# Small self-attention on packed probabilities: blocks of 32x32 turned on VectorE, products on parts of the TensorE array, and each result bank with its own counter

## The chip, the cores and the metric

The kernel runs on one core of one Trainium2 chip. Its engines are TensorE (PE, with its weight loads listed apart as PEld), VectorE (DVE), ScalarE (ACT), GpSimd (POOL) and SyncE (SP), each with its own instruction stream; they meet at semaphores, which are counters that one engine raises and another waits for. The metric is the time of one execution on the device, in microseconds (us). The kernel before takes 1611.82 us, the median of three runs (1604.68 to 1613.89).

## What is computed

A block of three layers on `x` (64 sequences of 32 rows, 256 wide), all in float32 at the interface:

```python
x = x + xattn(_layernorm(x), ctx_1024)   # 16 heads of 128, 257 keys for each sequence, rmsnorm on q and k
x = x + attn(_layernorm(x))              # 16 heads of 16, 4 key/value heads, rotary, causal over 32 rows
x = x + ffn(_layernorm(x))               # 8 experts, the best one for each row, plus a shared expert
```

The middle layer is the one that the change rewrites:

```python
scores = jnp.einsum('bqhgd,bkhd->bhgqk', qg, k) * scale
scores = jnp.where(causal, scores, -inf)
attn = jax.nn.softmax(scores, axis=-1)
y = jnp.einsum('bhgqk,bkhd->bqhgd', attn, v).reshape(bsz, seqlen, dim)
return ternary_linear(rms_norm(y), w_proj)
```

## The kernel before

The 2048 rows are worked on as 16 tiles of 128 rows, so a tile holds four sequences (`NB` = 4) of 32 rows. The program has a prologue (`pro`, which prepares weights and starts tile 0), 15 `full` periods, a `last` period and four `expert` periods. One full period does the early half of the next tile (cross attention) and the late half of this one (the end of the cross attention, the small self-attention, the shared expert, the routing). Each engine has a list of step names in `ORDER` for a period, and issues the steps in that order; nothing else sets the order. An engine waits at a step until its operands are counted as ready, and everything behind it on the same engine waits too.

The steps that matter here. `K0` to `K7` are the key products of the cross attention (12 matmuls of 512 columns each, into the four banks of `AB`); ACT squares two of the banks and DVE takes statistics of the other two. `Q`, `QP` and `f` are other large products. For sequence `b` of the tile: `rk{b}` turns and spreads the key norms into `C`; `s{b}` are its scores, into `AB`; `e{b}` (ACT) the exponentials; `i{b}` (DVE) the inverse sums; `n{b}` (POOL) scales the probabilities; `pt{b}` (PE) turns them into `C` and the last key's into `Db`; `ph{b}` and `tl{b}` (ACT) copy these out, `dp{b}` (DVE) writes the low half; `o{b}` (PE) is the product with the context, into `Eb`; `oh{b}` and `do{b}` drain it; `c{b}` (POOL) splits the context rows that `o{b}` multiplies. `h{b}` (POOL) splits the context that the next tile's `K` steps need, and `scat` (POOL) sends the tile's rows to the experts.

The small self-attention is `qk` (turns the heads), `sc` (16 products with 16 rows of contraction, of all 128 rows of the tile with all 128, of which only the four diagonal blocks of 32x32 are used), the mask on DVE (`sc`), the exponentials on ACT (`sc`), which write the four blocks of each head into `px`, a 128x2048 array that is zero elsewhere, `pt` (PE turns the 16 heads of `px`, 128x128 each, ACT and DVE copy them to `pxT`), `pv` (16 products of `pxT` with 17 columns, the last of which gives the sums), `yt` (turns `y`), and `pr` (the projection).

PSUM is divided into the four banks of `AB` (counters 0 to 3), `C` (two banks, one counter), `Db` and `Eb`. `filled` counts what PE has written there, `drained` what has been read out. Line 587 is the helper through which nearly all products go, line 924 the squares of the keys, line 1281 the statistics of the keys.

## Time and profile before

| | us |
|---|---|
| median of 3 runs | 1611.82 |
| lowest and highest | 1604.68, 1613.89 |
| the profiled execution | 1609.09 |
| its span, first to last instruction | 1607.3 |
| mean granted TensorE clock | 0.946 |

PE is busy for 86% of the span, DVE for 65%, ACT for 54% and POOL for 34%. A busy PE is not PE at its peak: the end of a matmul is modelled, and a matmul at half the clock is as busy as one at the full clock. The profile names for each idle time the engine that ended it.

### The profile page before, as it was taken

The page shows a single profiled execution, that of the slowest core. Times are in us where ns is not written, and L with a number is a line of the kernel's source. Part 1 is how long each engine was busy: PE and PEld are TensorE (multiplying, and loading weights), DVE is VectorE, ACT ScalarE, POOL GpSimd, SP SyncE. Part 2 cuts the span into 40 slices and gives each one's busy share as a digit, 9 for nine tenths or more (in the row PEclk, how much of TensorE's full clock was granted, in tenths as well). Part 3 has the DMA queues.
Part 4 walks back from the last instruction along what each step waited for, and adds up shares of the span by engine and source line. Part 5 has one row for each costly group of instructions (what it writes and reads, how often), then busy time and mean ns, then how long its engine had stood idle before and what let it go on. Part 6 is the DMA issues. An engine that isn't in the chain of part 4 may idle for free.

```text
span 1607.3 us, 32866 instructions
## 1 busy us (share of the span) xinstructions
PE 1378.4 (86%) x9178; PEld 956.8 (60%) x9178; DVE 1044.2 (65%) x3905; ACT 864.9 (54%) x3432; POOL 540.7 (34%) x1338
## 2 busy tenths in 40 slices
PE   5859989998989898989999998989898989955882
PEld 2635757565756666665757565756666665734661
DVE  6836767676767676777767676767676777733112
ACT  5455656566565656565565566565656565621110
POOL 2143333334243525243343334342525243300003
PEclk9989999999999999999998999999999999976896
DMA  9010000000000001010000000000101010100544
GB/s 372 4 28 8 26 17 21 13 27 13 24 17 14 27 10 30 10 30 7 24 17 21 13 25 15 24 17 10 30 10 30 7 33 3 59 6 19 163 127 134
DMA packets 41190, 59.63 MB, mean 37 GB/s; under 512 B 5094, under 2 KB 35953, under 8 KB 40096
## 3 DMA queue, kind: packets, MB, share of 16 engines
q1 hardware_dynamic: 36880, 50.73, 9.9%
q0 software_dynamic: 2064, 6.14, 1.2%
q10 hardware_dynamic: 2176, 2.10, 0.4%
q14 instruction: 59, 0.48, 0.1%
q8 instruction: 11, 0.18, 0.0%
HBM read 48.62 MB, written 10.49 MB: 37 GB/s over the span
## 4 chain that ended last, share of the span: by engine, by line
PE 57%; issue 14%; POOL 10%; DVE 9%; ACT 7%; DMA 3%; POOLq 1%; SPq 0%; DVEq 0%; ACTq 0%
PE AB L587 30%; PE Eb L587 9%; PE Db L587 5%; PE C L720 3%; PE C L587 3%; ACT px L1003 2%; DMA ctxn<-expert_rows 2%; POOL prob L1140 2%; PE AB L783 2%; POOL c_lo L1105 2%; PE C L704 2%; DVE sc L1509 1%; ACT AB L924 1%; POOL c_hi L1103 1%; POOL pjunk L1099 1%
## 5 line engine op out<-in xcount | busy, mean ns | idle before, releaser
L924 ACT ACTIVATE AB<-AB 128x128 f32<-128x128 f32 (+1 forms) x1160 | 302.8, 261 | 180.8 <-PE AB L587 175.8
L1099 POOL TENSOR_TENSOR pjunk<-pjunk 128x1 f32<-128x1 f32 x288 | 55.9, 194 | 703.2 <-DVE sinv L1443 341.3
L1281 DVE BATCH_NORM_STATS2 kst<-AB 128x6 f32<-128x256 f32 x512 | 182.1, 417 | 71.3 <-PE AB L587 64.9
L587 PE MATMUL AB<-wk_hi,c_hi 128*128 128x512 f16 x512 | 205.2, 401 | 20.8 <-DVE sc L1509 10.0
L924 ACT ACTIVATION_READ_ACCUMULATOR AB<-AB 128x1 f32 (+1 forms) x1160 | 215.4, 186 | 0.0
L587 PE MATMUL AB<-wk_lo,c_hi 128*128 128x512 f16 x512 | 204.0, 398 | 0.0
L587 PE MATMUL AB<-wk_hi,c_lo 128*128 128x512 f16 x512 | 203.0, 396 | 0.0
L993 ACT ACTIVATE prob<-prob,nbias,rq 128x257 f32<-128x257 f32 x256 | 150.6, 590 | 39.8 <-DVE nbias L1438 39.4
L1140 POOL TENSOR_SCALAR prob<-prob,sinv 128x257 f32<-128x257 f32 x256 | 123.8, 484 | 20.1
L587 PE MATMUL AB<-ctxT,qpT 128*128 128x257 f32 x512 | 127.3, 392 | 0.2 <-DVE kst L1281 0.2
L962 ACT CAST pT<-C 128x1024 f16<-128x1024 f32 x64 | 64.5, 1008 | 80.4 <-PE C L720 80.4
L587 PE MATMUL Eb<-pT,cn_hi 128*128 128x512 f16 x256 | 78.8, 390 | 33.6 <-DVE pT L1447 33.6
L587 PEld LDWEIGHTS AB<-ctxT,qpT 128*128 128x128 f32 x512 | 96.0, 196 | 16.6 <-DVE kst L1281 1.0
L720 PE MATMUL C<-consts_sb,prob 128*128 128x128 f32 x512 | 71.9, 286 | 38.4 <-POOL plast L1150 21.9
L587 PEld LDWEIGHTS AB<-wk_hi,c_hi 128*128 128x128 f16 x512 | 52.0, 102 | 88.2 <-issue 18.4
L1432 DVE CUSTOM_DVE_ANT_0 prob<-AB,rkb 128x257 f32<-128x257 f32 x256 | 96.2, 421 | 10.4 <-issue 9.2
L1116 POOL TENSOR_TENSOR rstd<-var,minus_half 128x1 f32<-128x1 f32 x64 | 35.3, 552 | 190.0 <-DVE var L1266 155.5
L587 PEld LDWEIGHTS AB<-wk_hi,c_lo 128*128 128x128 f16 x512 | 52.3, 102 | 67.2 <-issue 12.1
L720 PEld LDWEIGHTS C<-consts_sb,prob 128*128 128x128 f32 x512 | 58.8, 148 | 55.2 <-ACT rkb L987 23.7
L587 PE MATMUL Db<-wvo_hi,o_halves 128*128 128x256 f16 x512 | 88.2, 276 | 1.4 <-DVE o_halves L1453 1.4
L1447 DVE TENSOR_TENSOR pT<-C,pT 128x1024 f16<-128x1024 f32 x64 | 77.9, 1217 | 15.6 <-ACT pT L962 15.1
L587 PE MATMUL AB<-x_hi,wqk_hi 128*128 128x128 f16 x512 | 86.6, 219 | 0.0
(253 smaller groups left out, 3240.7 us busy)
## 6 DMA issues: line engine op xcount, KB each, us to landing
ctxT<-in_ctxT SPq DMA_DIRECT2D x64, 128.5 KB, 2.1
ctxn<-in_ctxn SPq DMA_DIRECT2D x64, 128.0 KB, 2.1
wq_hi<-in_w SPq DMA_DIRECT2D x4, 768.0 KB, 4.9
wq_lo<-in_w SPq DMA_DIRECT2D x4, 768.0 KB, 6.2
expert_rows<-base POOLq DMA_DIRECT2D x1, 2048.0 KB, 15.7
xin<-in_x SPq DMA_DIRECT2D x16, 128.0 KB, 2.2
prob<-in_wqT SPq DMA_DIRECT2D x1, 2048.0 KB, 19.1
xres<-in_x SPq DMA_DIRECT2D x16, 128.0 KB, 2.0
```

Source lines behind the costliest of these rows:

```text
L587: return pe.matmul(out, lhsT, rhs, start=start, stop=stop)
L704: ins = pe.transpose(C[:, g // 2, KT * P * (g % 2) + P * tt:KT * P * (g % 2) + P * (tt + 1)], rkx[:, b % 2, tt, P * g:P * (g + 1)], ident)
L720: ins = pe.transpose(C[:, tt, P * g:P * (g + 1)], prob[:, b, g, P * tt:P * (tt + 1)], ident)
L924: ins = nc.scalar.activation(k, k, ACT.Square, accum_out=sums[0:m, h:h + 1])
L962: nc.scalar.copy(pT[:, b % 2, 0].rearrange("p t n -> p (t n)"), C[:].rearrange("p a n -> p (a n)"))\
L993: ins = nc.scalar.activation(prob[:, b, g], prob[:, b, g], ACT.Exp, bias=nbias[:, b, g:g + 1], scale=rq[:, G * b + g:G * b + g + 1], accum ...
L1099: own.mark(pool.tensor_tensor(pjunk[:, 0:1], pjunk[:, 1:2], pjunk[:, 1:2], ALU.mult))
L1116: pool.tensor_tensor(rstd[:, n:n + 1], var[:, n:n + 1], minus_half[:], ALU.pow)\
L1140: ins = pool.tensor_scalar(prob[:, b, g], prob[:, b, g], sinv[:, b, g:g + 1], P_SCALE, ALU.mult, ALU.mult)
L1281: ins = V.bn_stats(stats[:, 0, 2 * half + n], AB[0:m, 2 + half, 2 * D * n:2 * D * (n + 1)])
L1432: V.tensor_tensor_reduce(prob[:, b, g], AB[:, g, 0:SKV], rkb[:, b % 2, g], 1.0, BELOW, ALU.mult, ALU.max, smax[:, b, g:g + 1]).then_inc(dr ...
L1447: V.tensor_tensor(all_of(pT[:, b % 2, 1]), all_of(C[:]), all_of(pT[:, b % 2, 0]), ALU.subtract)\
```

## The change

1. The probabilities are kept packed: `ex`, 128 rows by 16 heads by 32 keys (128x512, a part of `px`). One exponential writes them. DVE then sums them, divides them (before, the division came behind the product), and turns them with one instruction that transposes each 32x32 block (`step_sm`). The 16 turns on PE, the 128x512 copies of them and the zeros of `px` are gone.
2. `pv` is 16 products with 32 rows of contraction and 32 columns of weights over 128 columns, each on its own 32x32 part of the array: sequence `b` gives the rows and the bank, the key/value head `kv` the columns. The result is `y` already turned, so `yt` is gone. ACT copies it out (four copies) and squares it; DVE adds the squares of the four groups; PE sums over the rows (`st`); DVE and POOL make the norm's factor. Since 16 of every 32 rows of `y` turned are empty, `pr` has four products of 256 columns in place of two, and the weights `wproj` are laid out with gaps by the prologue (`wpad`).
3. `sc` issues its 16 products with the four groups of rows in turn (before: four products of one group, then the next).
4. The two banks of `C` have counters of their own, 4 and 5, and `rk`, `pt`, `qk`, `up` and their drains go bank by bank.
5. `o{b}`, `f` and `Q` first issue the products that need only the high halves, and wait for the low halves behind them.
6. The first two integer steps of `newton` become one.
7. The step lists are written anew.

```diff
 "PE":
-    K0 pt3 K1 K2 X K3 o3 Q f rk0 K4 xt1 K5 qkv QP K6 qk s0 rk1 sc K7 s1 pt pv pt0 s2 yt pr rk2 o0 pt1
-              xt2 s3 lg up pos o1 rk3 pt2 dn o2
+    K0 K1 K2 pt3 X K3 o3 Q f K4 rk0 xt1 K5 qkv QP K6 s0 qk sc rk1 K7 s1 pt0 pv pr st s2 rk2 o0 pt1 xt2
+              s3 lg o1 up pos rk3 dn pt2 o2
...
 "POOL":
-    h2 h0 h3 h1 n3 X r0 ln1 cl r1 c0 c2 c1 n0 r2 y n1 ln2 c3 r3 n2 scat
+    h0 h1 n3 X h2 c0 h3 r0 cl c1 r1 ln1 n0 r2 y n1 ln2 r3 c3 n2 scat c2
...
 (PE, attend)
                 for tt in range(KT):
+                    pe.wait_ge(ph_ready[tt].sem, ph_ready[tt].at(p, f"ph{b}"))
                     mm(Eb[:], cn_hi[:, b, tt], pT[:, b % 2, 0, tt], start=tt == 0, stop=False)
+                    mm(Eb[:], cn_lo[:, b, tt], pT[:, b % 2, 0, tt], start=False, stop=False)
+                for tt, s in enumerate("45"):
+                    pe.wait_ge(drained[s].sem, drained[s].at(p, f"pt{b}"))
                     mm(Eb[:], cn_hi[:, b, tt], pT[:, b % 2, 1, tt], start=False, stop=False)
-                    mm(Eb[:], cn_lo[:, b, tt], pT[:, b % 2, 0, tt], start=False, stop=False)
...
 (PE, step_pv)
-                for n, s in enumerate(BANKS):
-                    pe.wait_ge(drained[s].sem, drained[s].at(p, "pt"))
-                    for h in range(4 * n, 4 * n + 4):
-                        ins = mm(Eb[:, (AD + 1) * h:(AD + 1) * (h + 1)], pxT[:, h], vals[:, h % AKV])
+                probs = exT.rearrange("p i (kv q) -> p i kv q", kv=AKV)
+                for kv in range(AKV):
+                    for b, s in enumerate(BANKS):
+                        rows = slice(SQ * b, SQ * (b + 1))
+                        ins = mm(AB[SQ * kv:SQ * (kv + 1), b, 0:P], vals[rows, kv], probs[rows, :, kv])
...
 (ACT, step_sc)
-                for b in range(NB):
-                    rows = slice(SQ * b, SQ * (b + 1))
-                    ins = nc.scalar.activation(px[rows, :, SQ * b:SQ * (b + 1)], sc[rows], ACT.Exp)
+                nc.scalar.activation(all_of(ex), all_of(sc[:]), ACT.Exp).then_inc(ex_ready.sem, 1)
...
 (ACT, step_pv)
+                for b, s in enumerate(BANKS):
+                    act.wait_ge(filled[s].sem, filled[s].at(p, "pv"))
+                    ins = nc.scalar.copy(yT.rearrange("p i (b q) -> p b i q", b=NB)[:, b],
+                                         AB[:, b, 0:P].rearrange("p (i q) -> p i q", q=SQ))
+                    ins.then_inc(drained[s].sem, 1)
+                for s in BANKS:
+                    act.wait_ge(drained[s].sem, drained[s].at(p, "pv"))
+                nc.scalar.activation(all_of(ysq), all_of(yT), ACT.Square).then_inc(ysq_ready.sem, 1)
...
 (DVE, step_sm)
+                step(V.tensor_reduce(psum[:], by_key, AX.X, ALU.add))
+                step(V.reciprocal(prec[:], psum[:]))
+                step(V.tensor_tensor(by_key, by_key, prec[:].unsqueeze(2).broadcast_to([P, AH, SQ]), ALU.mult))
+                V.transpose(all_of(exT), all_of(ex)).then_inc(exT_ready.sem, 1)
```

How the order moves at three places. On PE in the middle of a full period, before: from the scores `s1` (the first row) over the turns of `px`, `pv` and `pt0` to the scores `s2`.

```order
L587 MATMUL AB<-ctxT,qpT 128x257 x4
L779 REGISTER_ALU
L781 REGISTER_ALU
L783 MATMUL AB<-consts_sb,px 128x128 x16
L789 REGISTER_ALU
L587 MATMUL Eb<-vals,pxT 128x17 x16
L715 REGISTER_ALU
L717 REGISTER_ALU x2
L720 MATMUL C<-consts_sb,prob 128x128 x8
L587 MATMUL Db<-ident,plast 12x128 x4
L587 MATMUL AB<-ctxT,qpT 128x257 x4
```

The same stretch of the changed kernel, from `s1` to `s2`.

```order
L593 MATMUL AB<-ctxT,qpT 128x257 x4
L729 REGISTER_ALU
L731 REGISTER_ALU
L733 MATMUL C<-consts_sb,prob 128x128 x8
L735 REGISTER_ALU
L593 MATMUL Db<-ident,plast 12x128 x4
L590 REGISTER_ALU
L593 MATMUL AB<-pxT,vals 32x128 x16
L816 REGISTER_ALU
L593 MATMUL Eb<-wproj,pxT 128x256 x4
L593 MATMUL Db<-ones,px 128x1
L593 MATMUL AB<-ctxT,qpT 128x257 x4
```

`pt0` has moved ahead of the small attention's product and now stands directly behind `s1`; `pr` and the sum of squares stand ahead of `s2`.

On ACT, in the same part of the period, before: from the exponentials of the small attention to the copy of `y` turned.

```order
L1003 ACTIVATE px<-sc 32x16x32 x4
L915 REGISTER_ALU
L916 COPY pxT<-AB 128x512 x2
L991 REGISTER_ALU
L993 ACTIVATE prob,ssum<-prob,nbias,rq 128x257 x4
L961 REGISTER_ALU
L962 CAST pT<-C 128x1024
L915 REGISTER_ALU
L916 CAST pTl<-Db 12x512
L915 REGISTER_ALU
L916 COPY yT<-Db 128x256
```

The same part of the changed kernel.

```order
L1023 ACTIVATE px<-sc 128x512
L1009 REGISTER_ALU
L1010 COPY rkb<-C 128x2x256 x2
L937 REGISTER_ALU
L938 CAST pTl<-Db 12x512
L984 REGISTER_ALU
L985 CAST pT<-C 128x512 x2
L1040 REGISTER_ALU
L1041 COPY pxT<-AB 128x4x32 x4
L1046 ACTIVATE px<-pxT 128x512
L1014 REGISTER_ALU
L1016 ACTIVATE prob,ssum<-prob,nbias,rq 128x257 x4
```

The exponentials `e1` of sequence 1 (the row with `prob,ssum`) have moved from ahead of the copies of `pT` to behind them and behind the copies and squares of `y`.

On PE at the end of a full period, before: from `rk3` over `pt2` and `dn` to the first products of `o2`.

```order
L704 MATMUL C<-consts_sb,rkx 128x128 x8
L717 REGISTER_ALU
L720 MATMUL C<-consts_sb,prob 128x128 x8
L587 MATMUL Db<-ident,plast 12x128 x4
L584 REGISTER_ALU
L587 MATMUL Eb<-sw,hT 128x256 x3
L728 REGISTER_ALU
L584 REGISTER_ALU
L735 REGISTER_ALU
L587 MATMUL Eb<-pT,cn_hi 128x512 x2
L587 MATMUL Eb<-pT,cn_lo 128x512
```

The same place of the changed kernel.

```order
L718 MATMUL C<-consts_sb,rkx 128x128 x8
L590 REGISTER_ALU
L593 MATMUL Eb<-sw,hT 128x256 x3
L731 REGISTER_ALU
L733 MATMUL C<-consts_sb,prob 128x128 x8
L593 MATMUL Db<-ident,plast 12x128 x4
L590 REGISTER_ALU
L747 REGISTER_ALU
L593 MATMUL Eb<-pT,cn_hi 128x512
L593 MATMUL Eb<-pT,cn_lo 128x512
L593 MATMUL Eb<-pT,cn_hi 128x512
L593 MATMUL Eb<-pT,cn_lo 128x512
```

`dn` (the row with `sw,hT`) now stands between `rk3` and `pt2`, and `o2` begins with the products of the high half.

## Rows read from the trace of the kernel before

**Rows 1.** The page: busy time of each engine, its share of the span, and its instructions.

```profile
PE 1378.4 (86%) x9178; PEld 956.8 (60%) x9178; DVE 1044.2 (65%) x3905; ACT 864.9 (54%) x3432; POOL 540.7 (34%) x1338
```

**Rows 2.** Instructions on `px`: count, duration in ns, first and last start in us.

```profile
L783 PE MATMUL AB<-consts_sb,px x256: 272/273/477, 179.2 to 1459.8; 128*128 128x128 f32 x128
```

**Rows 3.** Timeline of PE in one period: start, us, instruction, idle before and its releaser.

```profile
678.43 1.04 PE L766 MATMUL C<-consts_sb,heads 128*128 128x128 f32 x8
...
682.01 2.81 PE L587 MATMUL AB<-wt_q 16*128 16x128 f32 x32
...
692.02 1.97 PE L783 MATMUL AB<-consts_sb,px 128*128 128x128 f32 x16 [0.68 <-ACT px L1003]
693.82 3.64 PE L587 MATMUL Eb<-vals,pxT 128*128 128x17 f32 x32
697.31 1.07 PE L720 MATMUL C<-consts_sb,prob 128*128 128x128 f32 x8
...
701.31 1.13 PE L587 MATMUL Eb<-wproj,yT 128*128 128x256 f32 x4 [0.46 <-ACT yT L916]
...
704.71 1.06 PE L720 MATMUL C<-consts_sb,prob 128*128 128x128 f32 x8
```

**Rows 4.** Who PE waited for from 606.6 to 692 us, one period: us, times, longest.

```profile
PE Eb L587 <- DVE pT L1447: 1.9, 1, 1.9
PE C L720 <- ACT rkb L987: 1.1, 1, 1.1
PE Eb L596 <- DVE xn L1270: 1.0, 1, 1.0
...
PE AB L783 <- ACT px L1003: 0.7, 1, 0.7
PE C L720 <- POOL plast L1150: 0.6, 1, 0.6
```

**Rows 5.** Stretches of that period: length, busy time of the engines, granted clock, DMA.

```profile
686.00:688.00 2.00, 2.00 (x6) 0.64 (x5) 1.83 (x6) 1.04 (x9) 0.00 (x0) 0.50 0.00 0
...
694.00:696.00 2.00, 2.00 (x21) 2.00 (x20) 1.83 (x8) 2.00 (x7) 0.00 (x0) 1.00 0.54 177
```

**Rows 6.** Timeline of DVE from the mask of the small scores to `i0`.

```profile
683.82 3.63 DVE L1509 TENSOR_TENSOR sc<-AB,consts_sb 32x256 f32<-32x256 f32 x10 [1.19 <-PE AB L587]
...
688.31 0.69 DVE L1522 TENSOR_TENSOR sc<-sc,scm 128x512 f32<-128x512 f32 x1
689.03 1.43 DVE L1281 BATCH_NORM_STATS2 kst<-AB 128x6 f32<-128x256 f32 x4
690.37 0.16 DVE L1443 RECIPROCAL sinv<-ssum 128x4 f32<-128x4 f32 x1
```

**Rows 7.** Timeline of ACT: the copy of the turned heads, exponentials, copies of `pT` and `pTl`.

```profile
679.51 1.01 ACT L916 COPY wt_q<-C 128x1024 f32<-128x1024 f32 x1 [0.48 <-PE C L766]
...
695.58 0.59 ACT L993 ACTIVATE prob<-prob,nbias,rq 128x257 f32<-128x257 f32 x1
...
698.42 1.01 ACT L962 CAST pT<-C 128x1024 f16<-128x1024 f32 x1 [2.16 <-PE C L720]
699.33 0.57 ACT L916 CAST pTl<-Db 12x512 f16<-12x512 f32 x1
```

**Rows 8.** Timeline of POOL: the scaling of the probabilities (`n0`), and the next one's start.

```profile
690.90 2.15 POOL L1140 TENSOR_SCALAR prob<-prob,sinv 128x257 f32<-128x257 f32 x4
...
693.57 0.22 POOL L1150 TENSOR_TENSOR plast<-prob,plast 128x4 f16<-128x4 f32 x1
...
701.29 0.19 POOL L1099 TENSOR_TENSOR pjunk<-pjunk 128x1 f32<-128x1 f32 x1 [0.59 <-DVE sinv L1443]
```

**Rows 9.** Timeline of POOL at a period's end: a context split, the scatter.

```profile
620.16 0.67 POOL L1160 TENSOR_TENSOR cn_lo<-ctxn,cn_hi 128x256 f16<-128x256 f32 x1
...
630.92 1.12 POOL L1181 DMA_INDIRECT expert_rows<-xn,slot_s  x1 [0.58 <-issue]
```

**Rows 10.** Timeline of ACT in the last period: the four exponentials.

```profile
1454.13 2.54 ACT L1003 ACTIVATE px<-sc 32x512 f32<-32x512 f32 x4 [8.67 <-DVE sc L1522]
```

More of the change, by code:

```diff
@@ L763, in step_qk @@
                 pe.wait_ge(heads_ready.sem, heads_ready.at(p, "h"))
-                start(p, "qk")
-                for m in range(2 * AKV):
-                    ins = pe.transpose(C[:, m // 4, P * (m % 4):P * (m % 4 + 1)], heads[:, m], ident)
-                ins.then_inc(filled["C"].sem, 1)
+                for n, s in enumerate("45"):
+                    pe.wait_ge(drained[s].sem, drained[s].turn(p, "qk"))
+                    for m in range(AKV * n, AKV * (n + 1)):
+                        ins = pe.transpose(C[:, n, P * (m % 4):P * (m % 4 + 1)], heads[:, m], ident)
+                    ins.then_inc(filled[s].sem, 1)
```

270 lines of the change are left out of this document (144 added, 126 removed).

## The prediction

> **What bounds the kernel now.** I read the page first. PE is busy for 86% of the span, DVE for 65%, ACT for 54%, POOL for 34% [rows 1]. The turns of `px` come once in a tile, from 179.2 to 1459.8 us [rows 2]: 15 intervals of 85.4 us, so the full periods are 80% of the time, and what a period gains counts fifteen times. Then the waits of PE in one period [rows 4]: 1.9 for `pT`, 1.1 for `rkb`, 1.0 for `xn`, 0.7 for `px`, 0.6 for `plast` and a few smaller, 7 of 85 us. So PE is the bound, but narrowly: the reader should see that each of these waits is the end of a chain through DVE, ACT and POOL, and that work taken from PE becomes time only until the next chain is late. So I follow the chains.
>
> **PE's ledger.** In the timeline [rows 3] the turns of `px` run from 692.02 to 693.82 (1.8 us) and the old `pv` to 697.31 (3.5). With the turns of `y` (0.2) that is 5.5 us a period that go. The 16 products of `sc` take 2.81. DVE begins its mask, which needs the first 8 of them, at 683.82 [rows 6], so 8 take at most 1.8 us, 0.22 each; all 16 take 0.18 each, so the groups of rows overlap a little already where one follows the other. Issued in turn they should overlap throughout: between a quarter (16 x 0.22 / 4 = 0.9) and no change (2.8). I take 1.3, nearer the quarter, because of the overlap that the row shows. The new `pv` is 16 such products, with 32 columns of weights: 0.9 to 3.6 (the old `pv`'s pace, 32 entries of 0.11 us); I take 1.4 for the same reason. `pr` has four products of 256 columns for two: its row is 1.13, so it takes about 2.0, +1.0; `st` is 0.15. Ledger: -5.5 - 1.5 + 1.4 + 1.0 + 0.15 = -4.4 us a period, 66 us in fifteen.
>
> The TensorE page of the Trainium skill (Part 3, Packing small matmuls) gives 3.07 times the speed for four groups of rows. By that `sc` would take about 1.15 us, an estimate from the page, and the sum would move by 0.15 us a period.
>
> **Stage 1, `K0` to `K6`: gain 1.2.** `pt3` now stands behind `K2`, and POOL does `n3` behind two context splits in place of four: the 0.6 for `plast` goes. The 1.0 for `xn` is DVE arriving late at `f`; `do3` has moved behind `KN0` and `Q`, `newton` is one step shorter, `f` starts without waiting for the low halves, and `K4` rather than `rk0` plus `K4` stands behind it with the same length in all. I leave 0.4 of it. What DVE queues behind `do3` is `RQ`, which `i0` and the biases need much later.
>
> **Stage 2, from the end of `K6` (678.43) to `pt1` (704.71, so 26.3 us): gain 1.2, or a loss of 0.6.** Times are from the end of `K6`. `s0` now goes before `qk`, so `sc` has nothing to cover ACT's copy of the heads (1.01 in one piece [rows 7], now two, the first overlapped): PE stands about 0.8, `sc` starts at 3.4 (before 3.6) and is done at 4.8. The mask takes 3.6, the maximum and the subtraction 1.4, the statistics of `K7` 1.4, `i0` 0.16 [rows 6]: `i0` is done at 11.5, before 12.1. So the shorter `sc` is worth 0.6 here, not 1.5: the chain on DVE is the limit. POOL's `n0` takes 690.61 to 693.79, 3.2 [rows 8], so `pt0` can start at 14.8; PE has only `s1` to do until then and **stands idle for 2.8 us**, where before it stood 0.7. This is a new wait, and it eats most of the ledger. Meanwhile DVE does `step_sm`: the sum and the product are 128x512 like the row of 0.69, the reciprocal 0.2; the transposition is not in the trace; its bounds are one such pass (0.69) and two (1.4), and I take one, since it reads and writes 128x512 once. Then `s1` (2.2) ends at 16.1, when `pt0` does. With two passes `pv` would start 0.7 later.
>
> `pv` ends at 17.5. ACT first copies `pTl` and `pT` (0.57 and two halves of 1.01 [rows 7]), then the four banks of `y`: 1024 columns take 1.01 and 512 take 0.57, so 128 take 0.25, four 1.0 to 1.2. `pr` starts at 18.8: **another 1.3 of PE idle**. Then `pr` 2.0, `st` (the squares on ACT 0.6 and DVE's sum 0.7 are behind `pr` by then), `s2`, `rk2`, `o0`: 25.0. On ACT `e1` stands behind all this (squares to 19.4, then four exponentials of 0.59), `i1` at 22, and POOL's `n1` takes 3.2: `pt1` at 25.1. Two chains end together, against 26.3 before. That is the gain of 1.2.
>
> **The clock.** The granted clock is 0.50, the 1.2 GHz level, at 686 to 688 us in each period, behind the products of 16 rows, and 1.00 at 694 to 696, in the old `pv` [rows 5]. In the changed kernel the stretch from `s1` to `pr` holds 4.1 us of idle time, 8 turns and 16 products that use a sixteenth of the array each, less than what stood before the drop in `sc`. I expect a second drop there in each period. At half the clock `pt0` costs 1.3 more (all behind it moves), and `pr` and `s2` 0.5 beyond what the chain through `e1` hides: +1.8. The first drop stays, under `K7`, where DVE's mask is slower anyway.
>
> **Stage 3, from `pt1` to the next `K0`: gain 2.0.** 1.1 (`rkb`) goes since `dn` now covers ACT's copy. Of the 1.9 for `pT` most goes, as `o2` starts on the high halves. What is late next is POOL: `c2` (0.40 and 0.67 and a gate, 1.3 [rows 9]) now stands behind the scatter, `o2` needs it, and the scatter needs DVE's `up` and `pos`. From the end of `up` I count 2.2 to the slots, 2.1 to the scatter's end, 1.3 for `c2`, 1.5 for `o2`: 7.1. Before it was 10.4, of which `o1` (1.5) is now ahead of `up`. Gain 1.8 to 2.0, bounds 0 and 3.0 (both waits gone).
>
> **Outside the periods.** The last period is a bare chain at half the clock: one exponential for four (2.54 to about 0.65 [rows 10]), masks that start earlier (1.3), no turns of `px` and `y`, but `pr` takes 4 and the norm's factor comes 1.4 behind it: about -3. The prologue gains a zeroing, two copies and four turns on DVE and PE, +1 (0 to 3); the zeroing of `px` that POOL loses was beside other work. The experts are not touched.
>
> **Sum.** 1.2 - 0.6 + 2.0 = 2.6 a period, 39 in fifteen, and 2 outside: 1609.1 - 41 = 1568 in terms of the profiled execution. The median of the runs shown is 2.7 above that execution, so 1571.
>
> **Rivals.**
> *No second drop.* The old `pv` kept the full clock with 17 columns a product, and the wait for `pT` did not lower it. Then stage 2 gains 1.2, 4.4 in all: 66 + 2, 1543.
> *Narrow products that do not overlap.* All 16 loads and products run in a row: `pv` 3.6, so +2.2 from `pt0` to `pr`, half hidden where the clock's 1.8 is already partly under it; I count +1.5 a period: 1593. For it: the old `pv` ran at its loads' pace, 0.11 each. Against it: the 0.18 of `sc`. The same TensorE page (LDWEIGHTS) says that a load's time goes by its columns and not by its rows, which would speak for this in `sc`, where the columns stay 128; this trace shows loads of 16 rows, but in one group at a time.
> *The edits cancel.* If stages 1 and 3 give 0.6 in place of 3.2 (POOL's and DVE's chains late at `K0` and `xt1`), nothing is left: 1610.
> *Slower.* One mechanism: the path `pt0`, ACT's copies, `pv`, `e1`, `n1` carries both the serial products (+2.2) and half the clock over `pt0`, `pv`, `pr` and `s2` in two drops (+3.4 in place of 1.8), 3.8 more than in the forecast. It decides from 2.6 more. Then a period is 1.2 longer: +18 - 2, about 1627. For it: two new PE waits on this very path. Against: it needs both.
> *The whole ledger arrives.* Waits covered, 4.4 + 3.0 a period: about 1498. Against: the idle time before `pt0` is fixed by DVE and POOL.
>
> **How the numbers follow.** Forecast 0.45 (1571), no second drop 0.18 (1543), no overlap 0.14 (1593), cancel 0.09, slower 0.10, the whole ledger 0.04. The range 1538 to 1608 leaves out the ledger and the slower case and takes in the bound of stage 3 on both sides. A measurement here tells 0.5% (8 us). Faster by more than that: 0.45 + 0.18 + 0.14 + 0.04 and a little of the cancel case, 0.82; within 0.08; slower 0.10.
>
> **What would show it.** The pitch of a period (about 82.8; 81 without the second drop); the wait before `pt0` for `plast`, near 2.8; a wait of `pr` for ACT's copies, near 1.3; 16 products of `pv` in about 1.4 us and of `sc` in 1.3; a second stretch of granted clock 0.50 in each period between `pt0` and `s2`; the waits for `pT` and `rkb` at the period's end gone and one for `cn` in their place. The prediction is wrong if the pitch is over 85, or if PE does not wait before `pt0`.

## The result, and the profile after

The changed kernel takes 1627.61 us (median of 4 runs, 1625.00 to 1630.07), against 1609.78 us for the kernel before beside it. The ratio is 1.0112, with a 95% interval of 1.0076 to 1.0148: slower by 1.1%, where 1571 us was forecast. The profiled execution has a span of 1628.3 us and a mean granted clock of 0.917 (before 1607.3 and 0.946).

The page of the changed kernel, busy times, answers to [rows 1]:

```profile
PE 1321.8 (81%) x8990; PEld 885.9 (54%) x8990; DVE 1059.9 (65%) x3844; ACT 842.5 (52%) x3560; POOL 542.5 (33%) x1337
```

PE is busy for 57 us less, and the span is 21 us longer. So the work was taken off PE as planned and did not become time. The waits of PE in the whole run of the changed kernel (engine, tile and line, who ended the wait: us in total, times, longest):

```profile
PE C L733 <- POOL plast L1183: 61.7, 19, 6.6
PE Eb L602 <- DVE xn L1297: 39.0, 16, 2.6
PE Eb L593 <- ACT pxT L1041: 28.0, 16, 1.8
PE Eb L593 <- POOL cn_lo L1193: 21.4, 15, 1.5
```

and the same list of the kernel before:

```profile
PE Eb L587 <- DVE pT L1447: 33.6, 17, 2.6
PE C L720 <- POOL plast L1150: 21.9, 18, 5.9
PE Eb L596 <- DVE xn L1270: 18.2, 16, 2.5
...
PE C L720 <- ACT rkb L987: 16.5, 15, 1.1
```

The waits for `pT` and `rkb` are gone as forecast. Those for `plast` and `xn` have grown by 61 us together, the two below them in the list are new, and one for `wt_q` (16.9 us in all) as well. The granted clock over five periods, before and then after (stretch, length, busy time of PE, PEld, DVE, ACT and POOL with counts, clock, DMA share, GB/s):

```profile
333.00:755.00 422.00, 386.18 (x2653) 264.58 (x2651) 303.00 (x1173) 256.95 (x1050) 158.08 (x401) 0.98 0.07 19
```

```profile
333.00:755.00 422.00, 363.08 (x2575) 240.19 (x2574) 297.48 (x1112) 247.46 (x1062) 155.87 (x394) 0.93 0.06 19
```

A mean of 0.98 is 17 us of 422 at the lower level (1.2 GHz), 0.93 is 59 us. Before, each of these periods has one stretch at that level, under `K7`. In the changed kernel the clock under `K7` is 1.00 in every period, and the lower level comes in 9 of 15 periods behind the wait for `xn`, and in all of them from the wait in front of `pt0` on. Here is the changed kernel's second stage on PE, which answers to [rows 3] (start, duration, instruction, idle time before it and its releaser):

```profile
701.87 1.17 PE L593 MATMUL AB<-wt_q 16*128 16x128 f32 x32 [1.12 <-ACT wt_q L938]
702.98 1.09 PE L718 MATMUL C<-consts_sb,rkx 128*128 128x128 f32 x8
...
713.78 1.97 PE L733 MATMUL C<-consts_sb,prob 128*128 128x128 f32 x8 [3.24 <-POOL plast L1183]
715.67 0.59 PE L593 MATMUL Db<-ident,plast 128*12 128x128 f16 x4
716.20 0.73 PE L593 MATMUL AB<-pxT,vals 32*32 32x128 f32 x32
718.71 3.75 PE L593 MATMUL Eb<-wproj,pxT 128*128 128x256 f32 x8 [1.78 <-ACT pxT L1041]
722.26 0.43 PE L593 MATMUL Db<-ones,px 128*128 128x1 f32 x2
...
726.86 1.04 PE L733 MATMUL C<-consts_sb,prob 128*128 128x128 f32 x8
```

The narrow products are as quick as hoped: `sc` fell from 2.81 to 1.17 us, and the new `pv` takes 0.73. Around them PE stands: 3.24 in front of `pt0`, 1.78 in front of `pr`. From `pt0` to `pr` the clock is at its lower level:

```profile
719.00:721.00 2.00, 2.00 (x6) 1.55 (x6) 1.76 (x3) 2.00 (x8) 0.00 (x0) 0.50 0.00 0
```

so `pt0` takes 1.97 where `pt1` takes 1.04, and `pr` 3.75.

**Where the time went**, from the two timelines, in the period I followed. From `K0` to `Q`, 0.8 less. From `Q` to the end of `K6`, 3.1 more. From there to `pt1`, 29.2 against 26.3: 2.9 more. From `pt1` to the next `K0`, 15.5 against 17.7: 2.2 less. This period lost 3.0; they are not all alike. Over the 14 intervals from the first `Q` of a full period to the last the mean went from 85.9 to 87.5, 23 us in all; in this mean the four parts are 0.7 less, 2.5 more, 2.0 more and 2.1 less. Outside them the time up to that first `Q` is 3.2 longer, the stretch from the last `Q` to the last `dn` 8.0 shorter and the end behind it 2.5 longer: 2 us less, and the sum is the 21 of the spans. The 3.2 is not the change's: i0_first and dense_fill run the same program up to that point, and reach it 4.1 us earlier than the changed kernel and 0.9 earlier than the one before. The 2.5 at the end is no clearer (121.8 to 129.5 us over all the runs below, 126.7 before, 129.3 in the changed kernel). So the question is what `Q` to `K6` and `K6` to `pt1` lose.

### The profile page after: what moved, and what is told of

It is laid out like the page before. It is cut to its first block, busy times and chain, and to the rows that moved or that the text cites. A ratio compares the mean times of both kernels' runs of the same rounds, so it can differ in the third digit from the quotient of the medians.

```text
span 1628.3 us, 32714 instructions
## 1 busy us (share of the span) xinstructions
PE 1321.8 (81%) x8990; PEld 885.9 (54%) x8990; DVE 1059.9 (65%) x3844; ACT 842.5 (52%) x3560; POOL 542.5 (33%) x1337
## 4 chain that ended last, share of the span: by engine, by line
PE 36%; issue 22%; POOL 18%; ACT 7%; DVE 6%; DMA 3%; POOLq 1%; SPq 0%; DVEq 0%; ACTq 0%
PE AB L593 17%; PE Eb L593 7%; PE Db L593 5%; POOL prob L1173 4%; ACT AB L946 3%; PE C L733 3%; PE C L593 2%; POOL pjunk L1128 2%; DMA ctxn<-expert_rows 2%; POOL rkx L1164 2%; POOL c_lo L1134 2%; DVE sc L1544 1%; DVE kst L1308 1%; POOL c_hi L1132 1%; ACT pT L985 1%
## 5 line engine op out<-in xcount | busy, mean ns | idle before, releaser
L593 PE MATMUL AB<-wk_hi,c_hi 128*128 128x512 f16 x512 | 201.5, 394 | 28.4 <-DVE sc L1544 16.3
L593 PE MATMUL AB<-ctxT,qpT 128*128 128x257 f32 x512 | 134.6, 393 | 4.0 <-DVE kst L1308 3.2
L1173 POOL TENSOR_SCALAR prob<-prob,sinv 128x257 f32<-128x257 f32 x256 | 130.6, 510 | 20.2
L733 PE MATMUL C<-consts_sb,prob 128*128 128x128 f32 x512 | 77.9, 302 | 61.7 <-POOL plast L1183 61.7
L593 PEld LDWEIGHTS AB<-ctxT,qpT 128*128 128x128 f32 x512 | 91.6, 191 | 34.1 <-DVE kst L1308 14.7
L1010 ACT COPY rkb<-C 128x512 f32<-128x512 f32 x128 | 68.0, 583 | 78.7 <-PE C L718 78.7
L733 PEld LDWEIGHTS C<-consts_sb,prob 128*128 128x128 f32 x512 | 64.6, 154 | 79.4 <-issue 59.9
L593 PE MATMUL Eb<-pT,cn_hi 128*128 128x512 f16 x256 | 87.9, 384 | 22.9 <-POOL cn_lo L1193 21.4
L1483 DVE TENSOR_TENSOR pT<-C,pT 128x512 f16<-128x512 f32 x128 | 81.7, 677 | 10.9 <-ACT pT L985 10.9
L938 ACT CAST pTl<-Db 12x512 f16<-12x512 f32 x64 | 36.7, 573 | 100.5 <-PE Db L593 100.5
L593 PEld LDWEIGHTS AB<-wk_hi,c_lo 128*128 128x128 f16 x512 | 51.5, 101 | 64.7 <-issue 7.6
```

The lines of the kernel that those rows point to most:

```text
L593: return pe.matmul(out, lhsT, rhs, start=start, stop=stop)
L733: ins = pe.transpose(C[:, tt, P * g:P * (g + 1)], prob[:, b, g, P * tt:P * (tt + 1)], ident)
L938: nc.scalar.copy(out, in_).then_inc(drained[s].sem, 1)
L1010: nc.scalar.copy(rkb[:, b % 2, 2 * n:2 * n + 2, 0:KT * P], C[:, n].rearrange("p (g n) -> p g n", g=2)).then_inc(drained[s].sem, 1)
L1173: ins = pool.tensor_scalar(prob[:, b, g], prob[:, b, g], sinv[:, b, g:g + 1], P_SCALE, ALU.mult, ALU.mult)
L1483: V.tensor_tensor(pT[:, b % 2, 1, tt], C[:, tt], pT[:, b % 2, 0, tt], ALU.subtract).then_inc(drained[s].sem, 1)
```

## Experiments

All times are medians. The ratio is to the kernel before, run beside it, with its 95% interval. The kernel before took 1609.8 us beside the changed kernel; 1615.3 beside do3_first, i0_first, both_first and dense_fill; 1612.2 beside pool_ln1, pool_i0, pool_i0_do3 and order_old; 1618.6 beside c2_ahead, c2_fill, order_old_pt0 and sc_in_turn; 1611.4 beside before_st3, before_st3_pt0 and st2_old; 1614.8 beside counters_new and counters_old. So where two runs of different groups are set against each other in us, up to 9 us may be the group, and the ratios are the safer guide.

| run | us | ratio |
|---|---|---|
| the changed kernel | 1627.6 | 1.0112 (1.0076 to 1.0148) |
| do3_first | 1640.8 | 1.0166 (1.0101 to 1.0231) |
| i0_first | 1598.2 | 0.9891 (0.9823 to 0.9959) |
| both_first | 1613.0 | 0.9997 (0.9970 to 1.0023) |
| dense_fill | 1603.0 | 0.9918 (0.9889 to 0.9948) |
| pool_ln1 | 1589.5 | 0.9833 (0.9785 to 0.9882) |
| pool_i0 | 1562.1 | 0.9674 (0.9621 to 0.9726) |
| pool_i0_do3 | 1552.7 | 0.9627 (0.9576 to 0.9678) |
| order_old | 1638.7 | 1.0143 (1.0095 to 1.0191) |
| c2_ahead | 1548.6 | 0.9562 (0.9536 to 0.9588) |
| c2_fill | 1546.3 | 0.9542 (0.9511 to 0.9573) |
| order_old_pt0 | 1640.6 | 1.0129 (1.0102 to 1.0157) |
| sc_in_turn | 1616.6 | 0.9958 (0.9921 to 0.9996) |
| before_st3 | 1635.8 | 1.0152 (1.0122 to 1.0182) |
| before_st3_pt0 | 1680.9 | 1.0427 (1.0392 to 1.0461) |
| st2_old | 1566.2 | 0.9717 (0.9692 to 0.9742) |
| counters_new | 1588.6 | 0.9834 (0.9783 to 0.9885) |
| counters_old | 1635.1 | 1.0130 (1.0081 to 1.0178) |

### Two places in the lists, and the clock

**do3_first**, on DVE:

```
-K3 KN0 Q do3 RQ f K4
+K3 do3 KN0 Q RQ f K4
```

> The changed kernel with one step moved on DVE: the low half of o3 (do3) goes back ahead of the rotation's norms KN0, where it stood before. Theory A (stage 1 is lost to this order): the chain Q stats, RQ ends 0.7 us earlier against the start of Q, TensorE's wait for xn falls from 2.4 us to under 1.5 us per period, the clock drop of 3.4 us behind it goes in most periods, and the period falls by 1.5 to 2.5 us, which over 15 periods gives 1590 to 1605 us. Rival B (the newton chain is slow for another reason, POOL's work beside it, and do3 only fills a gap): the wait for xn stays above 2 us and the time within 0.4% of 1627 us.

Both times wrong: 1640.8, 13 us above the changed kernel, and the wait for `xn` rose from 39.0 to 52.4 us in the run. Of the two causes it is rival B's, POOL's work beside DVE, that holds, as the rest shows. The step between the statistics of `Q` and `xn` was gone and `xn` came later still. That sent me to DVE's small operations there. In the kernel before, one of `newton` (a timeline of DVE):

```profile
659.22 0.18 DVE L1255 SCALAR_TENSOR_TENSOR nb_<-nc_,nb_ 128x16 f32<-128x16 f32 x1
```

The same operations on the same 128x16 numbers in the changed kernel, on DVE, and what POOL does at the time:

```profile
675.62 0.53 DVE L1280 SCALAR_TENSOR_TENSOR nc_<-nb_ 128x16 f32<-128x16 f32 x1
676.18 0.17 DVE L1281 TENSOR_TENSOR nc_<-nc_,na 128x16 f32<-128x16 f32 x1
676.39 0.60 DVE L1282 SCALAR_TENSOR_TENSOR nb_<-nc_,nb_ 128x16 f32<-128x16 f32 x1
677.02 0.52 DVE L1280 SCALAR_TENSOR_TENSOR nc_<-nb_ 128x16 f32<-128x16 f32 x1
...
678.20 0.17 DVE L1281 TENSOR_TENSOR nc_<-nc_,na 128x16 f32<-128x16 f32 x1
```

```profile
675.42 0.69 POOL L1193 TENSOR_TENSOR cn_lo<-ctxn,cn_hi 128x256 f16<-128x256 f32 x1
...
676.35 1.16 POOL L1164 COPY rkx<-rk 128x512 f32<-128x512 f32 x2
...
682.80 0.56 POOL L1148 TENSOR_TENSOR rstd<-var,minus_half 128x1 f32<-128x1 f32 x1 [5.29 <-DVE var L1293]
```

POOL's last copy of `r1` ends at 677.51, and from then on every operation of DVE takes 0.17 again. In the list of before, `ln1` stands ahead of `cl` and `r1` on POOL, so POOL was waiting for DVE through all of this. The new list has `r0 cl c1 r1 ln1`, which fills POOL's wait with copies.

The durations say more. The slow operation that starts at 676.39 ends at 676.99, and the one at 677.02 ends at 677.54, where POOL's two copies end at 676.96 and 677.51. Over the whole run 45 of the 176 operations on 128x16 numbers take more than 0.3 us, and each of the 45 ends within 0.04 us of the end of an instruction of POOL. In do3_first it is 75 of 176, again each of them, and here DVE and POOL side by side:

```profile
677.24 0.89 DVE L1277 TENSOR_SCALAR nb_<-na 128x16 int32<-128x16 int32 x1
...
678.37 1.01 DVE L1281 TENSOR_TENSOR nc_<-nc_,na 128x16 f32<-128x16 f32 x1
```

```profile
677.04 1.05 POOL L1205 TENSOR_TENSOR cl_cast<-cl_cast,low_rows 12x512 f16<-12x512 f16 x1
678.17 1.18 POOL L1208 TENSOR_TENSOR cl_rows<-ctxl,cl_cast 12x512 f16<-12x512 f32 x1
```

So the small operation is not slower work: it stands until POOL's instruction is over. None of those that take under 0.3 us lies inside an instruction of POOL that takes over 0.3. The Trainium skill (SBUF — State Buffer, SBUF: two separate sides) says that a DVE instruction with two SBUF inputs contends with a GpSimd instruction that reads SBUF, and one in a two-port mode with any, for a pair of ports that one of them holds for a whole instruction. The rows agree with the whole instruction. Two inputs are not the condition here, since L1277 has one and took 0.89; whether it runs in a two-port mode no run shows.

**pool_ln1**, on POOL:

```
-h3 r0 cl c1 r1 ln1 n0
+h3 r0 ln1 cl c1 r1 n0
```

> The changed kernel with one step moved on POOL: ln1 goes ahead of cl, c1 and r1, where it stood before, so that POOL waits for the variance of ln1 while DVE works out the rotation's scale from the statistics of Q. Theory A (stage 1 is lost to POOL's copies beside DVE's small operations: 13 operations from the statistics of Q take 4.5 us here against 2.9 us before, and 5.8 us with do3 moved ahead, since POOL's work then falls on more of them): these operations take 0.17 us each again, xn is ready 1.5 us or more earlier, the wait for xn falls from 2.4 to under 1 us, the drop in stage 1 goes, and the time is 1590 to 1612 us. Rival B (DVE's operations are slow because TensorE or ACT read and write PSUM beside them): they stay slow, the wait stays, and the time within 0.4% of 1627 us.

Theory A, at the edge of its range: 1589.5, 38 us under the changed kernel from one word in a list. DVE's operations are at 0.17 to 0.18 again:

```profile
661.74 0.18 DVE L1282 SCALAR_TENSOR_TENSOR nb_<-nc_,nb_ 128x16 f32<-128x16 f32 x1
```

and PE's wait for `xn` over the run fell from 39.0 to

```profile
PE Eb L602 <- DVE xn L1297: 16.7, 16, 2.5
```

The 22 us of wait are not all of the 38: behind the wait for `xn` the clock fell for 3.4 us in 9 of 15 periods of the changed kernel (686 to 688 us: 0.50), and those stretches are gone too. The one behind `pt0` has grown for it, and in all a period has 9.8 us at the lower level where it had 10.7.

**i0_first**, on DVE, and **both_first**, with the edit of do3_first as well:

```
-K6 s0 sc K7 i0 sm s1
+K6 s0 i0 sc K7 sm s1
```

> The changed kernel with one step moved on DVE: the reciprocal i0 of block 0's sums goes ahead of the masks of sc, from behind the eighth K. Theory A (stage 2 is lost to DVE's order: i0 stands behind 5.2 us of masks and 1.4 us of statistics, so POOL starts prob of block 0 6 us later than its input allows, TensorE stands 3.2 us in front of pt0, and the clock falls for the 10.2 us behind it): the wait for plast of block 0 goes, the second drop is gone or only behind pr, the period falls by 3.5 to 5 us, and the time is 1550 to 1575 us. Rival B (TensorE then waits the same time for the transposed probabilities of sm, which DVE gives now 0.9 us later): the wait of 3.2 us turns into one of 2 to 2.5 us in front of pv, the clock falls anyway, and the time is 1610 to 1625 us.

> The changed kernel with both moves on DVE, do3 ahead of KN0 and i0 ahead of sc. If the two losses are independent, the gains add: 1515 to 1545 us. If they are one loss through the clock, which falls once per period in any case, the time is that of the better of the two alone, within 0.5%.

i0_first took 1598.2, 29 us under the changed kernel, between the two expectations, and each had a part of it. `pt0` starts without a wait, since `n0` is now done 3.9 us ahead of it. But PE then waits in front of `pv`:

```profile
693.95 1.04 PE L733 MATMUL C<-consts_sb,prob 128*128 128x128 f32 x8
694.92 0.39 PE L593 MATMUL Db<-ident,plast 128*12 128x128 f16 x4
697.41 0.51 PE L593 MATMUL AB<-pxT,vals 32*32 32x128 f32 x32 [2.10 <-DVE smax L1467]
699.06 3.75 PE L593 MATMUL Eb<-wproj,pxT 128*128 128x256 f32 x8 [1.14 <-ACT pxT L1041]
```

`pt0` and `pv` are at the full clock (1.04 and 0.51), `pr` still at half. The wait of 2.10 is for the banks of `s1`, at the end of one unbroken row of DVE's work from the masks on. both_first gave 1613.0, 15 us above i0_first, which neither expectation has: `do3` ahead of `KN0` did the same harm as before.

**dense_fill** tests the clock by itself, with the changed kernel's order:

```
+                if b == 0 and p.kind == "full":
+                    pe.wait_ge(drained["4"].sem, drained["4"].turn(p, "pt0"))
+                    for r in range(14):
+                        mm(C[:, 0], wk_hi[:, 0:P], wk_hi[:, 0:512])
                 pe.wait_ge(p_ready.sem, p_ready.at(p, f"n{b}"))
```

> The changed kernel with 14 additional products of 128x512, whose results are overwritten, in the bank of pt0 while TensorE waits in front of pt0 (14 x 0.215 = 3.0 us in a wait of 3.2 us). They do nothing but keep TensorE busy. Theory A (the idle stretch in front of pt0 is what takes the clock away for pt0, pv, pr and s2): the granted clock stays 1.00 over these steps, pt0 takes 1.0 us and pr 2 us instead of 2.0 and 3.8, the period falls by 2 to 4 us, and the time is 1570 to 1600 us although 14 products a period were added. Rival B (the drop is set by the narrow products of sc and pv themselves): the clock falls all the same and the time is 1625 to 1640 us.

```profile
696.73 3.19 PE L593 MATMUL C<-wk_hi 128*128 128x512 f16 x14
700.07 1.09 PE L737 MATMUL C<-consts_sb,prob 128*128 128x128 f32 x8
701.09 0.39 PE L593 MATMUL Db<-ident,plast 128*12 128x128 f16 x4
701.41 0.50 PE L593 MATMUL AB<-pxT,vals 32*32 32x128 f32 x32
703.92 2.58 PE L593 MATMUL Eb<-wproj,pxT 128*128 128x256 f32 x8 [2.02 <-ACT pxT L1045]
```

Theory A in its mechanism, and 3 us outside its range: 1603.0, 25 us faster with 14 useless products more in each period. `pv` is as narrow as before, and the clock stays. So what takes the clock away from `pt0` and `pv` is the idle stretch in front of them, and that costs about 1.6 us a period (25 in fifteen). What is left of half clock there is one stretch of 3.4 us, which begins inside `pr`.

**pool_i0** and **pool_i0_do3** put the edits together: ln1 and `i0`, then `do3` as well.

> The changed kernel with ln1 ahead of cl, c1 and r1 on POOL and i0 ahead of sc on DVE. If both gains count, the period is 83 to 84 us and the time 1565 to 1585 us. Rival (the period stays near 85.3 us, where before, i0_first and dense_fill all lie in spite of different work, because time that is taken out comes back as a further stretch at half clock): 1592 to 1600 us, as i0_first.

> The changed kernel with three moves: ln1 ahead of cl, c1 and r1 on POOL, i0 ahead of sc and do3 ahead of KN0 on DVE. Theory A (do3_first was slower only because it pushed the statistics' operations under POOL's work): with POOL out of the way do3's 0.7 us leave the chain to xn, and the time is 0 to 10 us under that of pool_i0. Rival B (do3 ahead of KN0 costs by itself, since it makes rk of the first half 2 us later for POOL): slower than pool_i0 by over 8 us, as do3_first against the changed kernel (13 us) and both_first against i0_first (15 us).

Both gains count nearly in full: 1562.1 is 65.5 us under the changed kernel, where 38.1 and 29.4 make 67.5 (by the ratios 4.4% of 5.0%). And `do3` ahead of `KN0`, which cost 13 and 15 us with POOL in the way, now gains 9: 1552.7. This is theory A of that run, and it settles stage 1: it is POOL's work that holds up DVE, and `do3_first` was slower only because it pushed DVE's chain further under them. The mean interval from `Q` to `Q` is now 82.6 us, where 82.8 was forecast.

### What of the change carries the gain

**order_old**: the changed kernel with every list in the order of before, as far as the steps exist in both. **order_old_pt0**: the same, with stage 2 as in i0_first. The core of the first:

```
-K6 s0 qk sc rk1 K7 s1 pt0 pv pr st s2 rk2 o0 pt1 xt2 s3 lg o1 up pos rk3 dn pt2 o2
+K6 qk s0 rk1 sc K7 s1 pv pt0 s2 pr st rk2 o0 pt1 xt2 s3 lg up pos o1 rk3 pt2 dn o2
```

> The changed kernel, its attention with compact probabilities included, with its steps on all four engines in the order of before as far as they exist in both (on TensorE pv, pt0, s2, pr, st; on ACT sc, pv, e1, ph0, tl0; on DVE i0, sm, s1, KN1, ys, dp0, i1, yv; POOL's list as before). Theory A (the loss is in the new order, the packed attention itself gains): the half clock behind pt0 is shorter, since pv stands in the wait for plast, the period is 82 to 84.5 us and the time 1560 to 1600 us. Rival B (the packed attention itself costs what the order cannot help: DVE's chain of masks, sum, reciprocal, product and transposition, then four copies and a square on ACT before pr): the period is 86 us or more, and the time 1620 to 1650 us.

> The kernel of order_old (1638.7 us) with the second stage alone in the new order and i0 ahead of sc: on TensorE pt0, pv, pr, st, s2, on ACT tl0, ph0, pv, e1, on DVE i0, sc, K7, sm. Stages 1 and 3 stay as before. Theory A (the packed attention needs other work in the time in which DVE makes its probabilities; with pt0 there it pays): the period falls from 88.7 to 84 to 86 us, and the time is 1570 to 1605 us. Rival B (the loss of order_old lies in the variance of y, which now stands behind pr and st and holds back n1, x2 and the rest in either order): 1620 to 1640 us.

1638.7 and 1640.6 are the times of rival B, but not a proof of its cause. Both kernels also have the counters per bank and the high halves first. These alone, with the old attention in the old order, take 1635.1 (counters_old, below): 1.0130 against 1.0143 for order_old, which can't be told apart. So in the old order the packed attention itself neither gains nor costs anything that these runs can tell. The periods are 88.7 us in both kernels and 88.2 in counters_old. In order_old the trace shows three places. In front of `pv` PE stands 3.31 us (for DVE, as in i0_first), and half clock follows. The variance of `y`, which DVE used to work out from `y` itself, now waits for `pr` and `st`: POOL's factor starts 51.5 us behind `Q` where it was 48.8, and `n1`, behind it on POOL, at 52.3 where it was 50.3. And in the next period PE waits for `n3`, and the clock falls once more:

```profile
744.11 0.38 PE L593 MATMUL Eb<-pT,cn_hi 128*128 128x512 f16 x1 [0.70 <-DVE base L1634]
...
750.87 1.97 PE L733 MATMUL C<-consts_sb,prob 128*128 128x128 f32 x8 [2.43 <-POOL plast L1183]
```

This third place does not come from the packed attention. counters_old has it too, though its `n1` stands 50.3 behind `Q` as before:

```profile
746.02 1.09 PE L727 MATMUL C<-consts_sb,prob 128*128 128x128 f32 x8 [2.39 <-POOL plast L1170]
```

In these two and in the kernel before POOL starts `n3` 6.4 us behind the scatter. PE starts `K0` 6.2 us behind it in the kernel before, and 4.3 in order_old and counters_old, since its wait of 2.0 for `pT` has become one of 0.7 for `base`. `pt3` stands directly behind `K0` in the old list, so the time saved there comes back as a wait for POOL.

**sc_in_turn**: the kernel before, with `sc` alone issued in turn over its groups of rows.

```
-                    for kv in range(AKV):
-                        ins = mm(AB[:, m, P * kv:P * (kv + 1)], headsT[rows, kv], headsT[rows, AKV + kv])
-                    ins.then_inc(filled[s].sem, 1)
+                for kv in range(AKV):
+                    for m, s in enumerate(BANKS):
+                        ins = mm(AB[:, m, P * kv:P * (kv + 1)], headsT[rows, kv], headsT[rows, AKV + kv])
+                        if kv == AKV - 1:
+                            ins.then_inc(filled[s].sem, 1)
```

> The kernel before with one part of the change alone: the 32 products of sc are issued over the four groups of rows in turn and all four banks are reported at the end. Theory A (the products overlap, but what follows sc is bound by DVE's masks, so the 1.6 us that TensorE saves are not saved on the path): sc takes 1.2 us instead of 2.8, the eighth K starts at most 0.5 us earlier, and the time is within 0.5% of before. Rival B (the time saved stays, and the half clock behind sc goes with the slow narrow products): the period falls by 1.5 to 3 us, 1565 to 1590 us. Rival C (the banks come all at the end, so the masks start later and the idle stretch behind sc grows): 1615 to 1635 us.

Theory A. First `sc` and the next `K7` in the kernel before, then in this one:

```profile
682.01 2.81 PE L587 MATMUL AB<-wt_q 16*128 16x128 f32 x32
685.47 0.61 PE L587 MATMUL AB<-wk_hi,c_hi 128*128 128x512 f16 x1 [0.65 <-DVE sc L1509]
```

```profile
688.38 1.17 PE L587 MATMUL AB<-wt_q 16*128 16x128 f32 x32 [0.32 <-DVE smax L1434]
691.29 0.53 PE L587 MATMUL AB<-wk_hi,c_hi 128*128 128x512 f16 x1 [1.74 <-DVE sc L1511]
```

The 1.6 us taken from `sc` came back as a longer wait for DVE's masks: `K7` starts 34.0 us behind `Q`, before 34.2. The clock still falls under `K7` (0.50 from 692 to 694 us), so the slow narrow products were not what lowered it in the kernel before. The ratio of 0.9958 is at the edge of what can be measured.

**before_st3** has the old attention and the new order of stages 1 and 3 (with `ln1` ahead of `cl`); **before_st3_pt0** has `i0` and `pt0` early as well; **counters_old** and **counters_new** add the counters per bank of `C` and the high halves first, in the old order and in that of before_st3. Of the lists of PE and POOL in before_st3:

```
-K0 pt3 K1 K2 X ... lg up pos o1 rk3 pt2 dn o2
+K0 K1 K2 pt3 X ... lg o1 up pos rk3 dn pt2 o2
-h2 h0 h3 h1 n3 X r0 ln1 cl r1 c0 c2 c1 n0 ... c3 r3 n2 scat
+h0 h1 n3 X h2 c0 h3 r0 ln1 cl c1 r1 n0 ... r3 c3 n2 scat c2
```

> The kernel before, with its own attention (turns of px, the old pv, yt), and with the steps of the first and third stage in the order of pool_i0_do3 (K0 K1 K2 pt3 at the period's start; lg, o1, up, pos, rk3, dn, pt2, o2 at its end; oh0 ahead of tl1; lg ahead of up on ACT; h0 h1 n3 and scat, c2 on POOL; ln1 ahead of cl). Theory A (the gain that stays is stage 3's order, 3.0 of 3.3 us a period, and the packed attention gives nothing): the period falls to 82 to 83 us and the time is 1550 to 1572 us, within 1% of pool_i0_do3. Theory B (the packed attention is needed: without it the new order meets a longer second stage, and the time comes back as half clock): 1590 to 1615 us.

> The kernel of before_st3 with stage 2 changed too, still with the old attention: i0 ahead of sc on DVE, pt0 ahead of the turns of px on TensorE, tl0 and ph0 ahead of the copies of px on ACT. Theory A (pt0 early fills the wait for px and costs nothing): 0 to 8 us under before_st3. Theory B (i0 delays the masks by 0.7 us, and the masks are what the turns of px wait for): 0 to 15 us above before_st3.

> The kernel of before_st3 (old attention, new order of stages 1 and 3 with ln1 ahead of cl) with the change's counters per bank of C and its products that start with the high halves. So it is the changed kernel in its mended form without the packed attention and without the new order of stage 2. Theory A (counters, high halves and stage 3's order together are the whole gain that stays; the packed attention gives nothing): the waits for pT and hT go, the period is 81.5 to 83 us, and the time 1540 to 1562 us, at or under pool_i0_do3's 1552.7. Theory B (the packed attention gives its share): 1570 to 1590 us, above pool_i0_do3 by over 1%.

> The kernel before, its attention and its order as they were, with the counters per bank of C and the products that start with the high halves alone. Theory A (in the old order nothing waits for the low halves, since other work stands between them, so finer counters find no wait to shorten): within 0.7% of before, 1600 to 1615 us. Theory B (they shorten waits in any order): 1570 to 1595 us.

Theory A fell in all four, and theory B holds in counters_new alone. The new order alone costs 1.5% (1635.8), and PE's waits in before_st3 say why:

```profile
PE Eb L587 <- DVE pT L1447: 47.7, 23, 2.8
PE C L704 <- DVE hT L1572: 21.2, 15, 1.4
```

With `o1` right behind `lg`, and `rk3` right behind `up`, PE meets the low half of `pT` and the second bank of `C` before they are done. The counters per bank and the high halves first take away these two waits (68.9 us; one of 21.4 for `c2` takes their place). Alone in the old order they cost 1.3% (1635.1: the wait for `pT` is gone, and that for `plast` is 46.2 us in place of 21.9, as above). Together they give 1588.6, 1.7% faster than before. So neither part would have been kept if tried alone. The packed attention takes the 1588.6 to 1566.2 (st2_old, below). In before_st3_pt0 `pt0` early with the old attention cost a further 45 us, three times the most that theory B allowed; its trace has PE waiting 32.1 us for `sc` on DVE, as theory B has it, against 12.5, and 10.2 us a period at the lower clock against 5.6. Which of its moves brings the clock down was not tested.

**st2_old**: pool_i0_do3 with stage 2 alone in the old order.

```
-K6 s0 qk sc rk1 K7 s1 pt0 pv pr st s2 rk2
+K6 qk s0 rk1 sc K7 s1 pv pt0 s2 pr st rk2
```

> The kernel of pool_i0_do3 with stage 2 alone in the old order (TensorE: qk, s0, rk1, sc, K7, s1, pv, pt0, s2, pr, st; ACT: sc, pv, e1, ph0, tl0; DVE: sc, K7, i0, sm). Theory A (the packed attention leaves TensorE without work between s1 and pv unless pt0 stands there; 3.3 us of idle, then half clock): the period rises by 1.5 to 3.5 us, 1575 to 1605 us. Rival B (the order of stage 2 does not matter once stages 1 and 3 are right; the loss of order_old was all in stage 3): within 0.5% of 1552.7 us.

1566.2, 13.5 us above pool_i0_do3 and 22 under counters_new: between the two expectations. The new order of stage 2 as a whole (`s0`, `rk1`, `i0`, `e1` and `yv` moved as well as `pt0`) is worth 0.9 us a period. The packed attention is worth 1.3 to 1.5 against counters_new (84.9 and 83.5 us a period; 22 us in fifteen); in that come the step less in `newton`, `sc` in turn, and `K4` ahead of `rk0`, which were not separated from it.

**c2_ahead** exchanges `c2` and `c3` on POOL (`r3 c2 n2 scat c3`), and **c2_fill** adds 9 and 4 dense products in the waits before `pv` and `pr`.

> The kernel of pool_i0_do3 with c2 and c3 exchanged on POOL, so that the halves of the context rows for o2 are made ahead of the scatter and not behind it. Theory A (TensorE's wait for cn_lo in front of o2, 21.4 us in the whole run, 1.4 a period, is a term of its own that the new order of the third stage added): that wait goes, the period falls by 1.0 to 1.4 us, and the time is 1530 to 1540 us. Rival B (the time comes back in front of pt3, K0 or o3, or the clock falls elsewhere): within 0.5% of pool_i0_do3's 1552.7 us.

> The kernel of c2_ahead with 9 additional products of 128x512 in front of pv and 4 in front of pr, whose results are overwritten (9 x 0.215 = 1.9 us in a wait of 2.1 us, 4 x 0.215 = 0.9 us in one of 1.1 us). Theory A (what half clock is left, 3.4 us in two of three periods behind these waits, goes when they are filled, and pr takes 1.9 instead of 2.8 us): 8 to 20 us under c2_ahead. Rival B (the products delay pv or pr by as much as the clock gives back, or the clock falls for another reason): within 0.4% of c2_ahead or above it.

c2_ahead is rival B: 1548.6, 0.3% under pool_i0_do3. The wait for `cn_lo` (21.4 us) is gone and one for `base` stands in its place,

```profile
PE Eb L593 <- DVE base L1634: 15.3, 15, 1.0
```

since `o2` also needs the bank that `dn` filled. c2_fill gave 1546.3, which can't be told from it, although its trace has only 0.7 us a period at the lower clock against 3.4. Its 13 products take 2.8 us a period, in waits that shrink by 2.3: with the waits mended, filling them gives back too little clock to pay. c2_ahead does only what the reference asks and beats both kernels, by 4.4% the one before and by over 5% the changed one (1548.6 and 1627.6 us).

## Why the prediction was wrong

**The ledger of PE was right, and cautious.** `sc` 1.17 where I took 1.3, `pv` 0.51 at the full clock where I took 1.4, `pr` 1.89 at the full clock (in order_old) where I took 2.0, the transposition one pass (0.71). The rival that narrow products do not overlap is refuted. In `pv` the trace shows 32 entries in 0.50 us, each on its 32x32 part. The Trainium skill (TensorE: Matmul & The Clock Gate, Part 3: Packing small matmuls) gives 3.07 for four groups of rows; from 0.22 us for one product I had made 1.15 for `sc` of it, an estimate, and the trace has 1.17. Against the 2.81 that `sc` took before, it is a factor of 2.4. The rule of the Trainium skill that a load's time goes by its columns (the same page, LDWEIGHTS) did not hold back `sc`, whose products still have 128 columns of weights.

**Stage 3, gain 2.0: right.** 2.2 was measured, with the waits for `pT` and `rkb` gone and the one for `c2` (1.42) in their place. What I did not see is that the order and the counters only work together.

**Outside the periods, 2: right in sum (2.3), and that is luck.** The bare chain of the last period gained 8.0 in place of 3. The 3.2 and 2.5 us lost at the two ends, which make up the difference, vary as much between kernels that are alike there. In the last period `sc` went from 5.13 to 2.09, at half clock both times.

**Stage 1, gain 1.2: the first step that failed.** The wait for `xn` rose to 2.4 us in place of my 0.4. I followed `do3` and `newton` on DVE and took each operation at its duration in the trace of before. That duration held only because POOL stood waiting for `ln1` there, in the same rows that I did not read. The change moved `cl`, `c1` and `r1` in front of `ln1`. DVE's chain between the statistics of `Q` and the scale became 1.6 us longer, beside 0.7 for `do3`, and the clock's drop behind the longer wait came on top. Shown by pool_ln1: 38 us. With that mended, `qkv` stands 17.9 us behind `Q` against 20.8 in the changed kernel and 18.0 before, and with the 0.8 from `K0` to `Q` stage 1 gains 0.9. With `do3` ahead as well (pool_i0_do3) it gains the 1.2 that I forecast.

**Stage 2, a loss of 0.6: the second.** The mechanism stood in the forecast: idle 2.8 before `pt0` (measured 3.2), 1.3 before `pr` (1.8), a second stretch of half clock between `pt0` and `s2`. Its size was wrong, 2.9 in place of 0.6. Two terms stand before `pt0`: the mask starts 0.7 later than I counted, since PE waits 1.12 for the heads with `rk1` no longer ahead of `sc`, and POOL's `n0` takes 0.6 more beside DVE. The third, about 1.4, is "`pr` and `s2` 0.5 beyond what the chain through `e1` hides". I took `e1`, `i1`, `n1` as a chain beside `pr`. In the new lists it is behind `pr`: DVE's `yv`, which stands ahead of `i1`, waits for `st`, and POOL's `y` stands ahead of `n1`:

```profile
722.72 0.16 DVE L1577 TENSOR_SCALAR var<-Db 128x1 f32<-128x1 f32 x1 [1.25 <-PE Db L593]
722.79 0.17 DVE L1478 RECIPROCAL sinv<-ssum 128x4 f32<-128x4 f32 x1
```

```profile
722.96 0.55 POOL L1148 TENSOR_TENSOR rstd<-var,minus_half 128x1 f32<-128x1 f32 x1 [3.96 <-DVE var L1577]
```

`e1` was done at 721.5, so `i1` stood 1.2 us behind a wait that is not its own. PE's own row has no idle time from `pr` to `pt1` either, and `n1`'s last operation ends at 726.67, 0.2 us before `pt1` starts. So nothing hid the 1.9 us that half clock added to `pr` (3.75 for 1.89). The rival called slower gave the measured time, 1627, and half of its mechanism: the clock, but not the serial products. The other half of the loss was stage 1, which it did not have, so that its number agrees is luck.

**The first drop: a third step, which cost nothing.** I let the drop under `K7` stay. It is gone in all 15 periods (granted clock 1.00 from 702 to 712 us), and the waits of stage 2 swallowed what that gave: `n0` waits for DVE, and not for `K7` on PE.

**The sum.** The forecast's period of 82.8 us was that of the changed kernel without these two faults (82.6 in pool_i0_do3). It was not that of the kernel as it stood: 87.5 in the mean, over the 85 that I had named as the sign of being wrong.
